# Layer 2 of a four-layer graph kernel: a ring of four quads of weight parts, and the group's inverses, scalings and finish one quad later

## The chip, the cores and the metric

One Trainium2 core runs the whole kernel. The metric is the device time of one execution in microseconds, the median of several runs. The engines are named PE (TensorE), DVE (VectorE), ACT (ScalarE), POOL (GpSimd) and SP (SyncE); each has its own queue of instructions and runs it in order, and they wait for each other by semaphores.

## The reference

Four layers over 4096 nodes with 256 features and a 4096 x 4096 0/1 matrix `adj`. Each layer takes `h = relu(layernorm(x))` and adds a graph layer to `x`. The change is in layer 2, counted from 0, a graph attention:

```python
h = x @ W
e = (h @ a[:D, 0])[:, None] + (h @ a[D:, 0])[None, :]
e = jnp.where(e > 0, e, 0.01 * e)
attention = jax.nn.softmax(jnp.where(adj > 0, e, MASK_VAL), axis=1)
x = x + jax.nn.elu(attention @ h)
```

Layer 3, which follows, is an attention with queries, keys and values made of the new `h`. Its projections are made in the finish of layer 2.

## The kernel before

The 4096 rows are eight groups (`G`) of 512 rows (`GW`), the 4096 columns 32 tiles of 128, taken four at a time: `R = 4` tiles are a quad, and a group has `Q = 8` quads. `aggregate` (line 1879) runs once for layer 1 and once for layer 2 (`weighted`). For layer 2 a quad of a group goes over three engines:

- DVE makes the weights of each of the four tiles in fp32 (`p32`, line 2033: a maximum, times the mask), for which it has four buffers;
- ACT copies each to fp16, the high part (`ph`, line 1983), and DVE subtracts for the low part (`pl`, line 2042, "lo" in the semaphores);
- PE multiplies 128-column pieces of both with the values `V`, also in two parts: for each tile 4 x 3 matmuls of 257 columns (lines 2113, 2114, 2116) into banks 0 to 3, one bank for each 128 rows of the group. Column 257 is the sum of the weights.

`ph` and `pl` have room for two quads: ACT's copy of a tile waits until PE has ended the same tile two quads before (line 1982). PE takes the last quad of a group by rows (`quad_by_rows`), so that bank 0 is complete first and bank 3 last.

When a group's sums are complete, DVE inverts the weights' sum of each bank (`inverse`, `rden`, line 2060) and ACT scales the bank into `ag` (line 2004). PE's first quad of the next group uses the same banks, and waits for `ag` of each bank (`act_s.before(g, "ag", i)` in `quad`). What follows is the finish, `finish_layer2`: `below` and `e` on ACT (the exponential of the negative part, lines 2413 and 2416), `pos` and `x` on DVE (2439, 2444) into `xo`, the moments for the layernorm (1853, 1857, 1859), `rstd` on POOL, `nb` (1871) on DVE, `h` on ACT (2184), its transposes on PE (211), their high part on ACT and low part on DVE (`hT`, 2178 and 2174), the projections on PE (`qT` and `v`, line 193), and their high and low parts again (`qT`, `v`, 2178 and 2174).

The finish of group g - 1 runs inside the loop over group g. The order is written out: in `groups` each engine does `quad(g, q)` and then `part(eng, g - 1, q)`, for q from 0 to 7, and the functions `act_part`, `dve_part`, `dve_middle` (between a quad's `p32` and its `lo`), `pe_part` and `sync` say with `if q == ...` which step belongs behind which quad. Before the change `inverse` and `ag` are behind quad 0 (the last bank's inverse inside quad 1, between its second and third `p32`); `below` at 0; `e`, `pos`, `x` and moments at 1; `nb`, `h` and the transposes at 2; `hT` at 4; the projections at 5; `qT` and `v` at 7. The last group's finish comes after the loop, with no quads between its steps. Group 0 comes before the loop, and in it ACT and DVE also make the two parts of `V` (lines 1996, 2047).

Of the kernel before, what the change touches and what calls it, by code (L numbers as in the profile page):

```python
# [21 lines left out]
F32 = mybir.dt.float32  # L22
F16 = mybir.dt.float16
# [8 lines left out]
P = 128  # L32
# [82 lines left out]
def build(nc, a, out):  # L115
# [20 lines left out]
    with top:  # L136
# [1746 lines left out]
        def aggregate(V, side, slope=None, wh=None):  # L1883
# [8 lines left out]
            v_at = v_row if weighted else v_own  # L1892
            with ExitStack() as mem, nc.Block() as block:
                mask = sb(mem, "mask", [P, MS, R * GW], U8)
                ph = sb(mem, "ph", [P, 2 * R, GW], F16)
                ag = sb(mem, "ag", [P, R * D], F32)
                rden = sb(mem, "rden", [P, R], F32)
                if weighted:
                    p32 = sb(mem, "p32", [P, R, GW], F32)
                    pl = sb(mem, "pl", [P, 2 * R, GW], F16)  # L1900
                    gam = sb(mem, "gam2", [P, T], F32)
                    dtil = sb(mem, "dtil", [P, T], F32)
                    red = sb(mem, "red", [P, 1], F32)
                    reded, d_spread, dmaxed, dtiled, lifted = (Count(sem(f"l2_{n}")) for n in (
                        "d_reduced", "d_spread", "d_max", "d_shifted", "s_lifted"))
                    omega_x, gam_x, v_x, omega_s, gam_s, v_col = (Count(sem(f"l2_{n}")) for n in (
                        "omega_exp", "gam_exp", "v_exp", "omega_scaled", "gam_scaled", "v_column"))
                    gam_spread, gam_rowed, v_hi, v_lo = (Count(sem(f"l2_{n}")) for n in (
                        "gam_spread", "gam_rowed", "v_hi", "v_lo"))
# [8 lines left out]
                masks = 16 * loaded[0]  # L1918

                def slot(q, r):  # L1920
                    return (q % 2) * R + r

                def mask_here(g, q):
                    return s_mask[q % MS], g * (16 * Q // MS) + (masks + 16 * (q // MS + 1))
# [48 lines left out]
                @block.scalar  # L1973
                def _(act):
                    def quad(g, q):
                        if not weighted:
                            act.wait_ge(*mask_here(g, q))
                        for r in range(R):
                            if weighted:
                                act.wait_ge(dve_q.sem, dve_q.at(g * Q + q, "p32", r))  # L1980

                            act.wait_ge(pe_q.sem, pe_q.before(g * Q + q, "pv", r, 2))
                            nc.scalar.copy(ph[:, slot(q, r), :], p32[:, r, :] if weighted else  # L1983
                                           mask[:, q % MS, r * GW:(r + 1) * GW]
                                           ).then_inc(act_q.sem, act_q.one("hi", r))

                    def gam_row(q):
                        act.wait_ge(gam_spread.sem, gam_spread.upto(q))
                        nc.scalar.copy(s_row[:, q * GW:(q + 1) * GW], bank[4 + q % R][:, :]).then_inc(gam_rowed.sem, 1)  # L1989

                    def make(q):

                        if q + 1 < Q:
                            gam_row(q + 1)
                        for t in range(q * R, q * R + R):
                            nc.scalar.mul(v_row(V, 0, t, D), wh[:, t * D:(t + 1) * D], vprime[:, t:t + 1]
                                          ).then_inc(v_hi.sem, 1)

                    def part(act, g, q):
                        if q == 0:  # L2000
                            work["sums_free"](act, g)
                            for r in range(R):
                                act.wait_ge(dve_s.sem, dve_s.at(g, "rden", r))
                                nc.scalar.mul(row(ag, r), bank[r][:, 0:D], rden[:, r:r + 1]
                                              ).then_inc(act_s.sem, act_s.one("ag", r))
                        work["act"](act, g, q)

                    if weighted:
                        act.wait_ge(dtiled.sem, dtiled.upto(0))
                        nc.scalar.activation(omega[:, :], dtil[:, :], ACT.Exp, scale=1.0 - slope  # L2010
                                             ).then_inc(omega_x.sem, 1)
                        act.wait_ge(lifted.sem, lifted.upto(0))
                        nc.scalar.activation(gam[:, :], gam[:, :], ACT.Exp, scale=slope - 1.0).then_inc(gam_x.sem, 1)
                        nc.scalar.activation(vprime[:, :], dtil[:, :], ACT.Exp, scale=slope).then_inc(v_x.sem, 1)
                        act.wait_ge(v_x.sem, v_x.upto(0))
                        nc.scalar.copy(v_column(V, 0), vprime[:, :]).then_inc(v_col.sem, 1)
                        gam_row(0)
                    groups(act, quad, part, make if weighted else None, work.get("act_between"), work.get("act_beside"))

                @block.vector  # L2020
                def _(dve):
                    def quad(g, q):
                        if not weighted:
                            return
                        n = g * Q + q
                        dve.wait_ge(*mask_here(g, q))
                        if isinstance(g, int):
                            dve.wait_ge(gam_rowed.sem, gam_rowed.upto(q))
                        for r in range(R):
                            dve.wait_ge(dve_q.sem, dve_q.before(n, "lo", r))  # L2030
                            if r == 2 and q == 1 and not isinstance(g, int):
                                inverse(g - 1, R - 1, R)
                            nc.vector.scalar_tensor_tensor(  # L2033
                                out=p32[:, r, :], in0=s_row[:, ds(g * GW, GW)],
                                scalar=omega[:, q * R + r:q * R + r + 1],
                                in1=mask[:, q % MS, r * GW:(r + 1) * GW], op0=ALU.max, op1=ALU.mult
                                ).then_inc(dve_q.sem, dve_q.one("p32", r))
                        if not isinstance(g, int):
                            middle(g - 1, q)
                        for r in range(R):  # L2040
                            dve.wait_ge(act_q.sem, act_q.at(n, "hi", r))
                            nc.vector.tensor_tensor(pl[:, slot(q, r), :], p32[:, r, :], ph[:, slot(q, r), :],  # L2042
                                                    ALU.subtract).then_inc(dve_q.sem, dve_q.one("lo", r))
                        if isinstance(g, int):
                            for t in range(q * R, q * R + R):
                                dve.wait_ge(v_hi.sem, v_hi.upto(t))
                                nc.vector.scalar_tensor_tensor(
                                    out=v_row(V, 1, t, D), in0=wh[:, t * D:(t + 1) * D], scalar=vprime[:, t:t + 1],
                                    in1=v_row(V, 0, t, D), op0=ALU.mult, op1=ALU.subtract).then_inc(v_lo.sem, 1)
# [17 lines left out]
                    def part(dve, g, q):  # L2067
                        if isinstance(g, int) or not weighted:
                            middle(g, q)
                        if q == 0:  # L2070
                            inverse(g, 0, R if isinstance(g, int) or not weighted else R - 1)
                        work["dve"](dve, g, q)

# [285 lines left out]


        def finish_layer2(mem, ag):
            xg = sb(mem, "xg4", [P, R * D], F32)
            xo = sb(mem, "xo2", [P, R * D], F32)
            e = w_gate[0][:, 0:2 * R * D].bitcast(F32)
            h = w_gate[1][:, 0:2 * R * D].bitcast(F32)
            qT = sb(mem, "qTg", [P, 2, K, GW], F16)
            stx, mvx, vex, rsx = stats_tiles(mem, "x2")
            nb = sb(mem, "nb4", [P, R], F32)
            pe_s.plan(("hT", K), ("qT", K), ("v", R))
# [38 lines left out]
                                    ).then_inc(s_xout, 16)  # L2408

            def act_part(act, g, q):  # L2410
                if q == 0:
                    act.wait_ge(act_s.sem, act_s.at(g, "ag", R - 1))
                    nc.scalar.activation(e[:, :], ag[:, :], ACT.Relu, scale=-1.0).then_inc(act_s.sem, act_s.one("below"))
                if q == 1:
                    act.wait_ge(act_s.sem, act_s.at(g, "below"))
                    nc.scalar.activation(e[:, :], e[:, :], ACT.Exp, scale=-1.0).then_inc(act_s.sem, act_s.one("e"))
                if q == 2:
                    normal(act, g, h, xo, nb, rsx)
                if q == 4:
                    act.wait_ge(pe_s.sem, pe_s.at(g, "hT", K - 1))  # L2420
                    hi(columns(kT[0], g), psum[:, 4:6, :], "hT", 0)
                if q == 7:
# [4 lines left out]
                    hi(own_values(0, g), made_values(), "v", 0)  # L2427

            def dve_middle(dve, g, q):
                if q == 2:  # L2430
                    shift(dve, g, nb, mvx, rsx, "nb", "rx")

            def dve_part(dve, g, q):
                if q == 1:

                    dve.wait_ge(act_s.sem, act_s.at(g, "ag", R - 1))
                    dve.wait_ge(s_xin, g * 16 + (first_in + 16))
# [7 lines left out]
                                                   op0=ALU.add, op1=ALU.add).then_inc(dve_s.sem, dve_s.one("x"))  # L2445
                    moments(dve, g, [(row(xo, r), None) for r in range(R)], stx, mvx, vex, ("xs", "xm", "xv"),
                            (dve_s.sem, dve_s.at(g, "x")))
                if q == 4:
                    dve.wait_ge(act_s.sem, act_s.at(g, "hT"))
                    lo(columns(kT[1], g), psum[:, 4:6, :], columns(kT[0], g), "hT", 0)  # L2450
                if q == 7:
# [3 lines left out]
                    lo(own_values(1, g), made_values(), own_values(0, g), "v", 0)  # L2455

            def pe_part(pe, g, q):
                if q == 2:

                    pe.wait_ge(dve_s.sem, dve_s.before(g, "v"))  # L2460
                    for k in range(K):
# [381 lines left out]
```

## Time and profile before

| | us |
|---|---|
| median of 3 runs | 2376.57 (2375.01 to 2377.3) |
| the profiled execution | 2376.45 |
| its span | 2374.8 |
| PE busy | 2227.9 (94%) |
| DVE busy | 1801.5 (76%) |
| ACT busy | 1373.3 (58%) |
| layer 2, first `p32` to last matmul into the sums | 1225.7 to 1645.8 |

The span is from the first to the last instruction. Busy time counts an engine's instructions; matmuls are pipelined, so that one matmul of 257 columns is listed with 0.27 us where the next starts 0.11 us later. A line of the timeline gives start, length, engine, line, operation, output and inputs with shapes, and in brackets the idle time before it and who ended it. Several like instructions in a row are merged (`x4`). The granted clock is 1.00 at 2.4 GHz and 0.50 at 1.2 GHz.

### The profile page before, as it was taken

The page shows a single profiled execution, that of the slowest core. Times are in us where ns is not written, and L with a number is a line of the kernel's source. Part 1 is how long each engine was busy: PE and PEld are TensorE (multiplying, and loading weights), DVE is VectorE, ACT ScalarE, POOL GpSimd, SP SyncE. Part 2 cuts the span into 40 slices and gives each one's busy share as a digit, 9 for nine tenths or more (in the row PEclk, how much of TensorE's full clock was granted, in tenths as well). Part 3 has the DMA queues.
Part 4 walks back from the last instruction along what each step waited for, and adds up shares of the span by engine and source line. Part 5 has one row for each costly group of instructions (what it writes and reads, how often), then busy time and mean ns, then how long its engine had stood idle before and what let it go on. Part 6 is the DMA issues. An engine that isn't in the chain of part 4 may idle for free. (4 is left out here: it accounts for less than half of the span.)

```text
span 2374.8 us, 45610 instructions
## 1 busy us (share of the span) xinstructions
PE 2227.9 (94%) x17180; PEld 1703.0 (72%) x17180; DVE 1801.5 (76%) x2845; ACT 1373.3 (58%) x2100; POOL 114.6 (5%) x124
## 2 busy tenths in 40 slices
PE   5899999999999998999978999997899999999998
PEld 4677767777677776888867888886356666666667
DVE  6967778696877855211259999997698898898896
ACT  6655564655646565666655555554365565565556
POOL 2000010010100001000000000000000000000000
PEclk9899999999999999999989999998999999999999
DMA  7542240414321112222211222221211111111000
GB/s 176 112 63 46 54 85 28 81 45 81 56 61 46 38 57 81 84 91 87 88 41 56 69 66 77 77 66 45 84 36 32 45 54 50 33 48 50 23 32 27
DMA packets 62934, 146.72 MB, mean 62 GB/s; under 512 B 10023, under 2 KB 14778, under 8 KB 61757
## 3 DMA queue, kind: packets, MB, share of 16 engines
q1 hardware_dynamic: 56461, 110.57, 14.8%
q0 software_dynamic: 5760, 33.56, 8.6%
q8 instruction: 100, 1.64, 0.3%
q10 hardware_dynamic: 560, 0.52, 0.1%
q14 instruction: 53, 0.43, 0.1%
HBM read 170.30 MB, written 41.43 MB: 89 GB/s over the span
## 5 line engine op out<-in xcount | busy, mean ns | idle before, releaser
L2113 PE MATMUL bank<-VB,ph 128*128 128x257 f16 x1936 | 487.6, 275 | 37.6 <-DVE pl L2042 19.9
L2114 PE MATMUL bank<-VB,ph 128*128 128x257 f16 x1936 | 486.6, 275 | 0.0
L193 PE MATMUL bank<-s_row,kT_hi 128*128 128x512 f16 x1024 | 305.5, 380 | 10.5 <-DMA s_row<-qT_d 8.6
L1559 PE MATMUL bank<-VA,ph 128*128 128x257 f16 x1024 | 280.8, 274 | 6.8 <-DVE VA L1168 6.8
L2770 PE MATMUL bank<-VA,w_dense 128*128 128x257 f16 x1024 | 280.7, 274 | 3.0 <-ACT w_dense L2631 2.4
L2116 PE MATMUL bank<-VB,pl 128*128 128x257 f16 x1024 | 281.4, 275 | 0.0
L1561 PE MATMUL bank<-VA,pl 128*128 128x257 f16 x1024 | 280.5, 274 | 0.0
L1560 PE MATMUL bank<-VA,ph 128*128 128x257 f16 x1024 | 280.5, 274 | 0.0
L2772 PE MATMUL bank<-VA,pl 128*128 128x257 f16 x1024 | 280.2, 274 | 0.0
L2771 PE MATMUL bank<-VA,w_dense 128*128 128x257 f16 x1024 | 280.1, 274 | 0.0
L1983 ACT CAST ph<-p 128x512 f16<-128x512 f32 x256 | 155.8, 617 | 153.5 <-DVE p L2033 144.1
L2113 PEld LDWEIGHTS bank<-VB,ph 128*128 128x128 f16 x1936 | 189.9, 98 | 69.2 <-DVE pl L2042 25.4
L811 ACT CAST ph<-p 128x512 f16<-128x512 f32 x256 | 153.2, 618 | 147.1 <-DVE p L1154 144.1
L2114 PEld LDWEIGHTS bank<-VB,ph 128*128 128x128 f16 x1936 | 190.7, 98 | 25.0
L193 PE MATMUL bank<-s_row,kT_lo 128*128 128x512 f16 x512 | 194.6, 380 | 0.0
L1154 DVE SCALAR_TENSOR_TENSOR p<-gamr,omega,mask 128x512 f32<-128x512 f32 x256 | 180.3, 747 | 2.5 <-ACT gamr L820 2.4
L193 PEld LDWEIGHTS bank<-s_row,kT_hi 128*128 128x128 f16 x1024 | 100.2, 98 | 110.9 <-DMA s_row<-qT_d 8.8
L2033 DVE SCALAR_TENSOR_TENSOR p<-s_row,omega,mask 128x512 f32<-128x512 uint8 (+1 forms) x256 | 175.8, 751 | 2.5 <-ACT s_row L1989 2.4
L1163 DVE TENSOR_TENSOR pl<-p,ph 128x512 f16<-128x512 f32 x256 | 165.0, 686 | 1.4 <-ACT ph L811 1.4
L2042 DVE TENSOR_TENSOR pl<-p,ph 128x512 f16<-128x512 f32 x256 | 159.9, 692 | 6.7 <-ACT ph L1983 6.7
L2607 ACT ACTIVATE s_row<-mask 128x1024 bf16<-128x1024 uint8 x128 | 134.1, 1053 | 34.3 <-DVE scores L2659 12.7
L1983 ACT CAST ph<-mask 128x512 f16<-128x512 uint8 x228 | 123.9, 622 | 8.8 <-DMA mask<-mask_d 5.1
(338 smaller groups left out, 4543.2 us busy)
## 6 DMA issues: line engine op xcount, KB each, us to landing
mask<-mask_d SPq DMA_DIRECT2D x256, 256.0 KB, 2.7
mask_d<-in_adj POOLq DMA_DIRECT2D x8, 2048.0 KB, 23.2
xg<-x SPq DMA_DIRECT2D x16, 512.0 KB, 4.3
x<-xo POOLq DMA_DIRECT2D x16, 512.0 KB, 3.0
xg<-in_x SPq DMA_DIRECT2D x8, 512.0 KB, 12.7
x<-xg SPq DMA_DIRECT2D x8, 512.0 KB, 3.9
qT_d<-qTg POOLq DMA_DIRECT2D x8, 512.0 KB, 2.9
s_row<-qT_d SPq DMA_DIRECT2D x8, 512.0 KB, 4.2
```

Source lines behind the costliest of these rows:

```text
L193: last = nc.tensor.matmul(out_ap, st, mv, start=(i == 0), stop=(i == len(todo) - 1))
L1154: nc.vector.scalar_tensor_tensor(out=p32[:, u % PR, :], in0=gamr[:, g % 2, :], scalar=omega[:, t:t + 1], in1=mask[:, n % MS, (u % R) * GW: ...
L1559: nc.tensor.matmul(acc, ph[:, u % HR, c], v_row(V, 0, t), start=(t == 0), stop=False)
L1560: nc.tensor.matmul(acc, ph[:, u % HR, c], v_row(V, 1, t), start=False, stop=False)
L1561: last = nc.tensor.matmul(acc, pl[:, u % HR, c], v_row(V, 0, t), start=False, stop=(t == T - 1))
L1983: nc.scalar.copy(ph[:, slot(q, r), :], p32[:, r, :] if weighted else mask[:, q % MS, r * GW:(r + 1) * GW]).then_inc(act_q.sem, act_q.one(" ...
L2113: nc.tensor.matmul(acc, p_hi, v_at(V, 0, t), start=first, stop=False)
L2114: last = nc.tensor.matmul(acc, p_hi, v_at(V, 1, t), start=False, stop=final and not weighted)
L2116: last = nc.tensor.matmul(acc, pl[:, slot(q, r), c], v_at(V, 0, t), start=False, stop=final)
L2770: nc.tensor.matmul(acc, ph[:, u % ring, j, c], v_row(V, 0, t), start=(t == 0), stop=False)
L2771: nc.tensor.matmul(acc, ph[:, u % ring, j, c], v_row(V, 1, t), start=False, stop=False)
L2772: last = nc.tensor.matmul(acc, pl[:, u % ring, j, c], v_row(V, 0, t), start=False, stop=(t == T - 1))
```

## The change

`ph` and `pl` of layer 2 get room for four quads, and ACT's copy waits for PE's tile of four quads before. `late = 1` moves `inverse` and `ag` behind quad 1, and the last bank's inverse into quad 2. In the finish, `below` goes to 1, where `e` already is; `pos`, `x` and moments to 2; `nb`, `h` and the transposes to 3; `hT` to 5. The projections (5) and `qT`, `v` (7) stay. `xg`, `xo` and `qT` have no tiles of their own any more and lie in a part of `w_dense` that is not used at that time. Layer 1 keeps its ring of two and its order.

```diff
+                ring = 4 if weighted else 2
+                late = 1 if weighted else 0
+                ph = sb(mem, "ph", [P, ring * R, GW], F16)
-                    pl = sb(mem, "pl", [P, 2 * R, GW], F16)
+                    pl = sb(mem, "pl", [P, ring * R, GW], F16)
                 def slot(q, r):
-                    return (q % 2) * R + r
+                    return (q % ring) * R + r
-                            act.wait_ge(pe_q.sem, pe_q.before(g * Q + q, "pv", r, 2))
+                            act.wait_ge(pe_q.sem, pe_q.before(g * Q + q, "pv", r, ring))
                     def part(act, g, q):
-                        if q == 0:
+                        if q == late:
                             work["sums_free"](act, g)
-                            if r == 2 and q == 1 and not isinstance(g, int):
+                            if r == 2 and q == 1 + late and not isinstance(g, int):
                                 inverse(g - 1, R - 1, R)
                     def part(dve, g, q):
-                        if q == 0:
+                        if q == late:
                             inverse(g, 0, R if isinstance(g, int) or not weighted else R - 1)
         def finish_layer2(mem, ag):
-            xg = sb(mem, "xg4", [P, R * D], F32)
-            xo = sb(mem, "xo2", [P, R * D], F32)
+            spare = dense_all[:, 2 * sizes[2]:2 * sizes[2] + 6 * R * D]
+            xg = spare[:, 0:2 * R * D].bitcast(F32)
+            xo = spare[:, 2 * R * D:4 * R * D].bitcast(F32)
-            qT = sb(mem, "qTg", [P, 2, K, GW], F16)
+            qT = spare[:, 4 * R * D:6 * R * D].rearrange("p (a k n) -> p a k n", a=2, k=K)
             def act_part(act, g, q):
-                if q == 0:
+                if q == 1:
                     act.wait_ge(act_s.sem, act_s.at(g, "ag", R - 1))
...
-                if q == 2:
+                if q == 3:
                     normal(act, g, h, xo, nb, rsx)
-                if q == 4:
+                if q == 5:
                     act.wait_ge(pe_s.sem, pe_s.at(g, "hT", K - 1))
             def dve_middle(dve, g, q):
-                if q == 2:
+                if q == 3:
                     shift(dve, g, nb, mvx, rsx, "nb", "rx")
             def dve_part(dve, g, q):
-                if q == 1:
+                if q == 2:
...
-                if q == 4:
+                if q == 5:
                     dve.wait_ge(act_s.sem, act_s.at(g, "hT"))
             def pe_part(pe, g, q):
-                if q == 2:
+                if q == 3:
...
```

## Rows read from the trace of the kernel before

**Rows 1.** Busy time by stretch: us, engines' busy (x instructions), clock, DMA
```profile
1388.10:1439.20 51.10, 48.67 (x430) 41.74 (x429) 48.83 (x84) 27.99 (x45) 2.60 (x3) 1.00 0.22 72
```
**Rows 2.** Waits, layer 2: who waited for whom, us, times, longest
```profile
PE bank L2113 <- DVE pl L2042: 19.9, 8, 3.0
DVE rden L2060 <- PE bank L2116: 13.9, 11, 3.6
...
ACT ph L1983 <- PE bank L2116: 2.5, 1, 2.5
```
**Rows 3.** Timeline of PE, round that begins at 1391.63 (group 3)
```profile
1391.63 0.28 PE L2113 MATMUL bank<-VB,ph 128*128 128x257 f16 x1
...
1401.11 0.27 PE L2116 MATMUL bank<-VB,pl 128*128 128x257 f16 x1
1403.81 0.28 PE L2113 MATMUL bank<-VB,ph 128*128 128x257 f16 x1 [2.43 <-DVE pl L2042]
...
1431.06 0.27 PE L2113 MATMUL bank<-VB,ph 128*128 128x257 f16 x1
```
**Rows 4.** Timeline of DVE, the same round
```profile
1389.46 0.17 DVE L2060 RECIPROCAL rden<-bank 128x1 f32<-128x1 f32 x1 [1.07 <-PE bank L2116]
...
1393.20 2.50 DVE L2042 TENSOR_TENSOR pl<-p,ph 128x512 f16<-128x512 f32 x4 [0.82 <-ACT ph L1983]
1395.62 1.22 DVE L2439 SCALAR_TENSOR_TENSOR xo<-ag,xg 128x1024 f32<-128x1024 f32 x1
...
1400.34 2.74 DVE L2033 SCALAR_TENSOR_TENSOR p<-s_row,omega,mask 128x512 f32<-128x512 uint8 x4
```
**Rows 5.** Timeline of ACT, the tail after the last group
```profile
1646.80 1.06 ACT L2413 ACTIVATE w_gate<-ag 128x1024 f32<-128x1024 f32 x1
1647.88 1.06 ACT L2416 ACTIVATE w_gate<-w_gate 128x1024 f32<-128x1024 f32 x1
```
**Rows 6.** Timelines of DVE, ACT and PE, border of groups 0 and 1
```profile
1280.38 2.74 DVE L2033 SCALAR_TENSOR_TENSOR p<-s_row,omega,mask 128x512 f32<-128x512 uint8 x4
...
1285.44 0.43 DVE L2060 RECIPROCAL rden<-bank 128x1 f32<-128x1 f32 x3
...
1285.63 1.20 ACT L2004 ACTIVATE ag<-bank,rden 128x256 f32<-128x256 f32 x3 [1.80 <-DVE rden L2060]
1287.34 0.47 ACT L2004 ACTIVATE ag<-bank,rden 128x256 f32<-128x256 f32 x1 [0.50 <-DVE rden L2060]
...
1286.71 0.27 PE L2116 MATMUL bank<-VB,pl 128*128 128x257 f16 x1
...
1287.86 0.28 PE L2113 MATMUL bank<-VB,ph 128*128 128x257 f16 x1
```
**Rows 7.** Timelines of PE, ACT and DVE at `v`, round of group 1
```profile
1328.94 0.27 PE L2113 MATMUL bank<-VB,ph 128*128 128x257 f16 x1
...
1329.23 1.01 ACT L2178 CAST VA<-bank 128x1024 f32 x1 [1.71 <-PE bank L193]
...
1330.45 1.23 DVE L2174 TENSOR_TENSOR VA<-bank,VA 128x1024 f32 x1 [1.11 <-ACT VA L2178]
1331.59 2.73 DVE L2033 SCALAR_TENSOR_TENSOR p<-s_row,omega,mask 128x512 f32<-128x512 uint8 x4
```
**Rows 8.** Timeline of PE, group 7: the gated matmul and the last
```profile
1595.87 0.28 PE L2113 MATMUL bank<-VB,ph 128*128 128x257 f16 x1
...
1645.78 0.27 PE L2116 MATMUL bank<-VB,pl 128*128 128x257 f16 x1
```
**Rows 9.** Busy time by stretch after holes of PE (clock after POOL), and PE's timeline
```profile
1300.10:1303.50 3.40, 3.40 (x17) 2.41 (x18) 3.40 (x6) 2.81 (x6) 0.00 (x0) 0.51 0.44 137
1352.75:1356.15 3.40, 3.40 (x31) 3.03 (x32) 3.40 (x6) 2.81 (x6) 0.00 (x0) 1.00 0.46 145
...
1300.54 0.42 PE L2113 MATMUL bank<-VB,ph 128*128 128x257 f16 x1
1300.75 0.42 PE L2114 MATMUL bank<-VB,ph 128*128 128x257 f16 x1
```

More of the change, by code:

```diff
@@ L1894, in aggregate @@
                 mask = sb(mem, "mask", [P, MS, R * GW], U8)
-                ph = sb(mem, "ph", [P, 2 * R, GW], F16)
+                ring = 4 if weighted else 2
+                late = 1 if weighted else 0
+                ph = sb(mem, "ph", [P, ring * R, GW], F16)
                 ag = sb(mem, "ag", [P, R * D], F32)
```

## The prediction

> **What bounds it now.** I read three kinds of view, in this order. The page and the busy times by stretch come first: in one round of layer 2 (51.1 us: eight quads of one group, with the finish of the group before between them) PE is busy 48.67 us and DVE 48.83 us, ACT only 27.99 us [rows 1]. Two engines are both nearly full, so which of them waits, and where, decides. Next, the waits: of the whole stretch of layer 2 the largest one of PE's matmuls is for the low parts, 19.9 us in 8 waits, and DVE's largest is `rden` for PE, 13.9 us [rows 2]. Last the timelines of one round, engine by engine. PE stops once a round, from 1401.22 (one matmul pitch of 0.11 after the last) to 1403.81, 2.59 us, before the low parts of quad 2 [rows 3]. DVE is late there because in that quad it has computed `pos`, `x` and the moments (1395.62 to 1400.34, 4.72 us) [rows 4]. And DVE itself stood idle 1.07 us at the third `rden` (PE had not ended that row) and 0.82 us before the low parts of quad 1, where ACT's copies were behind `ag` and `below` [rows 4]. So the round is one closed chain of both engines: PE from quad 2 to the end of quad 7, DVE from the inverses to the low parts of quad 2. The matmul let go by the fourth `ag` starts at 1391.63 in group 3 and at 1595.87 in group 7 [rows 3, 8]: 204.24 us for four rounds, 51.06 each. PE alone would need 51.06 - 2.59 = 48.47.
>
> **The change, part by part.**
>
> (1) Ring of four quads. It adds no instruction. What it lifts is ACT's wait for PE before a high part: 2.5 us, one time, in the whole layer [rows 2], on an engine with 23 us of idle time a round. Worth nothing by itself; what it makes possible is that DVE and ACT run further ahead of PE.
>
> (2) `inverse` and `ag` one quad later. The same four reciprocals and four scalings, but now queued on DVE behind the four `p32` and four `lo` of quad 1 (5.06 us, 1280.38 to 1285.44 [rows 6]), and on ACT behind the high parts of quad 1. Who waits: PE's quad 0 of the next group accumulates into the same banks 0 to 3 and waits for `ag` bank by bank; only `dve` and `act` are moved, not the sums' place. So PE can't begin quad 0 before DVE has ended quad 1. Before, its wait there was too short for the list of waits. This is an added wait of PE, and all of quads 0 to 7 is queued behind it.
>
> (3) The finish one quad later. `pos`, `x`, moments go from quad 1 to 2 on DVE, the transposes from 2 to 3, `hT` from 4 to 5; the projections stay in quad 5, `qT` and `v` in quad 7. Same instructions, so no work is added. `below` moves into quad 1 beside `e`, and both now stand ahead of the high parts of quad 2. Before, `below` alone did. `e` waits for `below`, and starts 1.08 us after it in the tail, where nothing is between them (1646.80 and 1647.88) [rows 5]; that much later the high parts start. DVE's 0.82 us idle becomes 1.90.
>
> (4) `xg`, `xo`, `qT` in the spare part of `w_dense`: same shapes, same instructions, 0. SP's load of `xg` and POOL's stores keep their place; SP runs four quads ahead of DVE, so that load is still issued before it is wanted.
>
> **The new round, step by step.** D is the start of the first reciprocal. In group 1, where nothing held DVE up, the first reciprocal (1285.44) to PE's matmul that waits for the fourth `ag` (1287.86) took 2.42 us [rows 6]; call that matmul the gate.
> - Gate to the first matmul of quad 6, after the projections: 1391.63 to 1431.06, less the stall of 2.59: 36.84 us [rows 3]. The stall is gone: DVE has done quad 2 long before.
> - ACT takes `v` 0.29 us after that matmul (1328.94 to 1329.23), DVE's `lo` of `v` 1.22 later (1330.45): the one round in which DVE waited for them [rows 7].
> - DVE then goes on 1.14 us later (1331.59) with the `p32` of quad 0 [rows 7], and two quads of `p32` and `lo` take twice 5.06, 10.12 us [rows 6]. Here is the next D.
>
> Sum: 2.42 + 36.84 + 0.29 + 1.22 + 1.14 + 10.12 = **52.03 us a round**, against 51.06. Is another chain longer? DVE by itself: 51.06, less the 1.07 us for which it waited in the inverses [rows 4], and 1.08 more for ACT: 51.07. So DVE comes to `v` 0.96 us too early and waits. PE by itself: 48.47. The chain over both is the longest. A check of PE against DVE within the round, counted from D: PE's quads are 48 matmuls of 0.11, 5.3 us, and nine of the first stand before the gate, so quad 3 starts at 2.4 - 1.0 + 3 x 5.3 = 17.3. DVE needs 2.8 + 0.3 us for `p32` and inverses and 1.9 idle to the low parts of quad 2, 2.4 for these, 4.7 for the finish (both [rows 4]) and 2.7 for the next `p32`: low parts of quad 3 from 14.8. They are 2 us ahead of PE, and in quads 4 and 5 DVE gains 0.2 more each. So PE has no stall inside the group.
>
> **From rounds to the end of the layer.** D of group 1: `p32` of quad 0 starts at 1280.38 [rows 6] and two quads take 10.12: 1290.50, gate at 1292.92. Before, it was 1287.86. Six rounds: 1292.92 + 312.18 = 1605.10 is the gate of group 7, then PE needs 1645.78 - 1595.87 - 2.59 = 47.32 us to its last matmul [rows 8]: 1652.42, before 1645.78. **+6.6 us.** The tail (last inverse, finish of group 7) is in the same order as before, 0, with some 1.7 us either way for the clock, below.
>
> **PE's clock.** The change turns a hole of 2.4 us into one of 52.03 - 2.42 + 0.71 - 47.32 - 0.27 = 2.73 us (0.71 from D to the first matmul: 0.19 to `ag`, 0.52 to PE [rows 6]), with 0.6 us more before the gate. After ten holes of 2.4 to 3.0 us the granted clock of the next 3 to 4 us was 0.50 to 0.58 (1.2 GHz all or most of the time) four times, from 1232, 1280, 1300 and 2323 us, and 1.00 (2.4 GHz) six times, in the six steady rounds [rows 9] (one of the four and one of the six stand there). In the low stretch 17 matmuls stand 0.21 apart instead of 0.11 [rows 9]: 1.7 us. No row says why some holes are followed by a fall, and the new ones are no shorter. I take the ratio, four in ten, of six holes: 2.4 x 1.7 = 4.1 us, bounds 0 and 10.2. The first hole is longer: PE ends quad 7 of group 0 at 1286.98 [rows 6] and would start at 1291.21, 4.2 us. I expect a low stretch, partly hidden by the waits for `ag`: 1.0, bounds 0 and 1.9.
>
> **Sum:** 6.6 + 4.1 + 1.0 = +11.7 us. The profiled execution took 2376.45 (span 2374.8 and 1.65 around it), 0.12 under the median 2376.57, so its like after the change is 2388.15, a span of 2386.5, and the median 2388.3 us.
>
> **Rivals.**
> - A, the forecast: 2388.3, own range 2384 to 2393. 56%.
> - B, the chain as above, but the clock stays: +6.6 to +7.3, 2383.5. For it: six steady holes in a row without a fall. Against: the two just before them fell. 16%.
> - C, a fall after every hole: 6.6 + 10.2 + 1.9 = +18.7, 2395.3. 10%.
> - D, the way over `v` is shorter than I make it (PE goes through its matmuls a microsecond faster, or DVE's lead is larger) and only DVE's own chain is left: 6 x 51.07 gives the gate of group 7 at 1599.34, +3.5, less the 2.59 of the last round: +0.9, 2377.5. 11%.
> - E, the other side: the hole of PE goes and none comes in its place, 7 x 2.59 = 18 us, 2358.5. The mechanism would be that DVE has a lead of more than two quads at the group's border, so that `ag` is ready when PE ends quad 7. The point from which this decides: DVE's work with its waits in a round must be under PE's 48.47 us. It is 51.07, of which 48.83 is bare work [rows 1], and any lead is lost each round. 7%, for what I can't see, half gains included.
>
> For E speaks a rule of the Trainium skill, Perfetto Trace Analysis, section Optimization Strategy: the same bubble repeating on an engine that should be saturated can mean that there are too few buffers for the next tile. The bubble here does repeat in all seven rounds [rows 2, 3], and by the rule a deeper ring would take it away and give 2358.5. But the rows name DVE's work, not a buffer, as what ends it.
>
> **Numbers.** A run of this kernel can tell about 0.2% (4.75 us) from no change, so slower is above 2381.3. A, B and C are slower but for a part of B's lower edge: 0.80. D is the same, with some of B: 0.13. Faster is E: 0.07. The range 2379.5 to 2395.5 holds A, B, C nearly whole and leaves out D and E.
>
> **What would show it.** After the change: no PE idle before quad 2; in its place PE idle of about 2.7 us before quad 0 of every group, ended by ACT `ag`; `rden` no longer waiting for PE inside the loop; DVE idle of about 1.9 us before the low parts of quad 2, ended by ACT `ph`; DVE `lo` of `v` waiting about 1 us for ACT (more after a low clock); rounds of 52.0 us at a clock of 1.00, and some of 53.7 with a stretch at half of it. Step 2 is wrong if PE's idle before quad 0 is absent; the sum is wrong if the `v` wait is absent (then D); and if rounds are below 49 us, E holds.

## The result, and the profile after

The changed kernel takes 2389.3 us (median of 5 runs, 2387.71 to 2390.97), the kernel before 2376.57 (median of 5, 2375.01 to 2378.76). The ratio is 1.0054, with a 95% interval of 1.0043 to 1.0066: slower by 12.7 us. The profiled execution took 2389.3 with a span of 2387.6 us, 12.8 more than before's 2374.8. The forecast was 2388.3 us, with a span of 2386.5.

The first view is the page of the changed kernel; its lines answer to the table ahead of the prediction.

```profile
span 2387.6 us, 45610 instructions
PE 2233.9 (94%) x17180; PEld 1704.2 (71%) x17180; DVE 1800.5 (75%) x2845; ACT 1373.7 (58%) x2100; POOL 114.6 (5%) x124
L2115 PE MATMUL bank<-VB,ph 128*128 128x257 f16 x1936 | 489.4, 276 | 44.1 <-ACT ag L2006 26.1
```

The count of instructions is the same and the busy times are nearly so: no work was added. What changed is who ends PE's idle time before the matmuls of the sums. Before, it was DVE's low parts [rows 2]; now it is ACT's `ag`. (Lines were added to the kernel, so L2113 of before is L2115, L2116 is L2118, L2042 is L2044, L2060 is L2062, L2004 is L2006, and the high and low parts of `qT` and `v`, L2178 and L2174, are L2180 and L2176. A tile that is now listed as `w_dense` is one of the three that moved there: `xg`, `xo` or `qT`.)

Next, one round of the changed kernel that has no low clock in it, from the first reciprocal of group 4 to that of group 5 (1449.43 to 1501.26 us, 51.83). The waits in it that matter here, with us in total, times, longest:

```profile
PE bank L2115 <- ACT ag L2006: 3.0, 2, 2.7
ACT ag L2006 <- DVE rden L2062: 2.1, 2, 1.8
DVE pl L2044 <- ACT ph L1985: 1.9, 1, 1.9
ACT VA L2180 <- PE bank L193: 1.5, 1, 1.5
DVE VA L2176 <- ACT VA L2180: 0.8, 1, 0.8
```

Against [rows 2], `rden` does not wait for PE any more and PE does not wait for `pl`. The new waits are the four that were said: PE for `ag`, DVE for `ph`, and DVE for `v` with ACT's wait for PE ahead of it. Their places are seen in the timelines of PE, ACT and DVE, in this order:

```profile
1450.15 0.28 PE L2115 MATMUL bank<-VB,ph 128*128 128x257 f16 x1 [2.73 <-ACT ag L2006]
...
1451.67 0.28 PE L2115 MATMUL bank<-VB,ph 128*128 128x257 f16 x1 [0.29 <-ACT ag L2006]
...
1488.50 0.27 PE L2115 MATMUL bank<-VB,ph 128*128 128x257 f16 x1
...
1488.79 1.01 ACT L2180 CAST VA<-bank 128x1024 f32 x1 [1.51 <-PE bank L193]
...
1449.43 0.29 DVE L2062 RECIPROCAL rden<-bank 128x1 f32<-128x1 f32 x3
...
1490.00 1.22 DVE L2176 TENSOR_TENSOR VA<-bank,VA 128x1024 f32 x1 [0.82 <-ACT VA L2180]
1491.14 2.73 DVE L2035 SCALAR_TENSOR_TENSOR p<-s_row,omega,mask 128x512 f32<-128x512 uint8 x4
...
1501.26 0.29 DVE L2062 RECIPROCAL rden<-bank 128x1 f32<-128x1 f32 x3
```

Read it as the chain of the prediction, where D is the first reciprocal and the gate is PE's matmul that waits for the fourth `ag`: D at 1449.43, the gate at 1451.67 (2.24 us), the first matmul of quad 6 at 1488.50 (36.83), ACT at `v` at 1488.79 (0.29), DVE at 1490.00 (1.21), the `p32` of quad 0 at 1491.14 (1.14), the next D at 1501.26 (10.12). The sum is 51.83.

The seven rounds do not all look like this. The first reciprocals of the eight groups start at 1289.51, 1343.45, 1396.06, 1449.43, 1501.26, 1553.08, 1606.45 and, after the loop, 1652.33 us: rounds of 53.94, 52.61, 53.37, 51.83, 51.82 and 53.37, then 45.88 with nothing of a next group behind it. The long ones begin with a stretch of low clock (the column after POOL's), at 0.50 or 0.52:

```profile
1290.20:1295.70 5.50, 5.48 (x26) 3.87 (x27) 3.59 (x8) 5.12 (x9) 0.00 (x0) 0.50 0.17 48
1344.20:1347.00 2.80, 2.80 (x14) 1.98 (x15) 2.25 (x5) 2.42 (x5) 0.00 (x0) 0.52 0.00 0
1398.10:1401.50 3.40, 3.20 (x16) 2.25 (x17) 1.49 (x3) 3.34 (x6) 0.00 (x0) 0.50 0.26 77
1450.15:1453.50 3.35, 3.06 (x26) 2.26 (x27) 2.27 (x5) 2.97 (x5) 0.00 (x0) 1.00 0.00 0
1502.00:1505.40 3.40, 3.11 (x27) 2.30 (x28) 2.25 (x5) 3.02 (x5) 0.00 (x0) 1.00 0.00 0
1555.10:1558.50 3.40, 3.18 (x15) 2.24 (x16) 1.49 (x3) 3.34 (x6) 0.00 (x0) 0.50 0.26 76
1607.20:1610.60 3.40, 3.11 (x27) 2.30 (x28) 2.24 (x5) 3.02 (x5) 0.00 (x0) 1.00 0.00 0
```

From the first `p32` to the end of the last matmul into the sums, layer 2 took 420.36 us before (1225.69 to 1646.05) and 431.57 now (1224.70 to 1656.27): +11.2. It began 1.0 us earlier, and what lies behind it took 731.4 instead of 728.7, +2.7. These two make up the rest of the 12.8.

### The profile page after: what moved, and what is told of

The parts are those of the page before. It is cut to its first block and busy times, and to the rows that moved or that the text cites. A ratio compares the mean times of both kernels' runs of the same rounds, so it can differ in the third digit from the quotient of the medians.

```text
span 2387.6 us, 45610 instructions
## 1 busy us (share of the span) xinstructions
PE 2233.9 (94%) x17180; PEld 1704.2 (71%) x17180; DVE 1800.5 (75%) x2845; ACT 1373.7 (58%) x2100; POOL 114.6 (5%) x124
## 5 line engine op out<-in xcount | busy, mean ns | idle before, releaser
L2115 PE MATMUL bank<-VB,ph 128*128 128x257 f16 x1936 | 489.4, 276 | 44.1 <-ACT ag L2006 26.1
L2116 PE MATMUL bank<-VB,ph 128*128 128x257 f16 x1936 | 488.1, 276 | 0.0
L2118 PE MATMUL bank<-VB,pl 128*128 128x257 f16 x1024 | 283.2, 277 | 0.0
L2115 PEld LDWEIGHTS bank<-VB,ph 128*128 128x128 f16 x1936 | 190.4, 98 | 77.8 <-ACT ag L2006 31.2
L2116 PEld LDWEIGHTS bank<-VB,ph 128*128 128x128 f16 x1936 | 191.3, 99 | 25.6
L2044 DVE TENSOR_TENSOR pl<-p,ph 128x512 f16<-128x512 f32 x256 | 159.3, 682 | 14.3 <-ACT ph L1985 14.3
## 6 DMA issues: line engine op xcount, KB each, us to landing
xg<-in_x SPq DMA_DIRECT2D x8, 512.0 KB, 12.6
```

The lines of the kernel that those rows point to most:

```text
L2115: nc.tensor.matmul(acc, p_hi, v_at(V, 0, t), start=first, stop=False)
L2116: last = nc.tensor.matmul(acc, p_hi, v_at(V, 1, t), start=False, stop=final and not weighted)
L2118: last = nc.tensor.matmul(acc, pl[:, slot(q, r), c], v_at(V, 0, t), start=False, stop=final)
```

## The experiments

The theory is that a round is the chain D, gate, PE to the projections, `v` on ACT and DVE, two quads on DVE, and that PE's low clock lengthens it. The rivals: the ring's depth matters by itself; the high parts that ACT makes late, behind `below` and `e`, set the round; the later steps of the finish cost, not the later inverses.

**The ring alone** (`ring_only`). Against the changed kernel the late inverses are undone, and in the finish every step that was moved goes back by one (`below`, `h` and `hT` on ACT; `nb`, the step with `x`, and `hT` on DVE; the transposes on PE). Each is an edit like the second pair of lines:

```diff
-                late = 1 if weighted else 0
+                late = 0
...
-                if q == 1:
+                if q == 0:
                     act.wait_ge(act_s.sem, act_s.at(g, "ag", R - 1))
```

> The ring of four quads and the moved tiles alone, with inverse, ag and every step of the finish where they were before. My theory: the ring hides nothing, since PE's hole before quad 2 is ended by DVE's work. The hole of 2.4 us stays in every round, rounds of 51.06, and the time is that of before, 2376.6 (within 2 us). Rival (too few buffers make the hole): the hole goes, rounds near 48.5, 2358.5.

Measured: 2376.34 us, ratio 1.0002 (0.9993 to 1.0011). Rounds of 51.06, as before, and the hole is in its place. PE's waits in the layer:

```profile
PE bank L2115 <- DVE pl L2044: 20.1, 8, 3.1
```

Against 19.9 us in 8 waits [rows 2]. Two more quads of buffers and the three moved tiles are worth nothing alone. With this falls the reading that the repeated bubble comes of too few buffers, which the Trainium skill, Perfetto Trace Analysis, section Optimization Strategy, names as a possible cause. Here the bubble stayed, and `late_undone` below makes it shorter by another order.

**`below` and `e` out of the way** (`exp_later`):

```diff
             def act_part(act, g, q):
-                if q == 1:
+                if q == 2:
                     act.wait_ge(act_s.sem, act_s.at(g, "ag", R - 1))
...
-                if q == 1:
+                if q == 2:
                     act.wait_ge(act_s.sem, act_s.at(g, "below"))
```

> The changed kernel with below and e behind the high parts of quad 2 instead of ahead of them. My theory (the round is the chain gate, PE to the projections, v on ACT and DVE, two quads on DVE): DVE's 1.91 us idle before the low parts of quad 2 goes, DVE's wait for v grows by the same, the clean round stays 51.8 and the time stays 2389 (within 2.5). Rival (ACT's wait is what lengthens the round): rounds of 49.9, 6 x 1.9 = 11 us less, 2378.

Measured: 2388.45 us, ratio 1.0055 (1.0041 to 1.0068); clean rounds of 51.83. The waits of the one from 1394.03 to 1445.86:

```profile
PE bank L2115 <- ACT ag L2006: 3.0, 2, 2.7
...
DVE VA L2176 <- ACT VA L2180: 1.7, 1, 1.7
DVE w_dense L2176 <- ACT w_dense L2180: 1.1, 1, 1.1
```

DVE's 1.9 us before the low parts of quad 2 is gone, and as much has come at `v` (0.8 to 1.7) and at `qT` (0 to 1.1; the line with `w_dense`). So that visible wait could go without shortening the round: the chain over PE set it. In this run's profile two of the six steady holes were followed by a low clock, not three, and not the same ones: its long rounds are the first (53.87), the fourth (53.40) and the last (47.44 instead of 45.88).

**The projections one quad earlier** (`project_earlier`):

```diff
             def pe_part(pe, g, q):
...
-                if q == 5:
+                if q == 4:
                     pe.wait_ge(dve_s.sem, dve_s.at(g, "hT"))
```

> The changed kernel with PE's projections behind quad 4 instead of quad 5, so that v is ready 5.3 us earlier. My theory: DVE no longer waits for v (0.8 to 1.7 us a round before), DVE's own chain is left, clean rounds of 51.0, and a low clock of PE costs nothing inside the loop, since DVE no longer waits for PE: 6 x 0.8 + about 4 = 9 us less than the changed kernel, 2380.5 (2378 to 2385). Rival (ACT's wait alone sets the round): no change, 2389.

Measured: 2376.66 us, ratio 1.0001 (0.9992 to 1.0010), which is no difference from the kernel before and 12.6 us less than the changed one. Rounds: 50.90, then five of 50.93. The direction and the round were right (51.0), but the time is below my range of 2378 to 2385. The changed rounds add up to 316.94 us and these to 305.55, 11.4 less, where I had put 9: the low clock in the changed rounds cost 6.0 and not 4. The stretch behind the layer, 728.7 instead of 731.4, does the rest. The waits of the round from 1442.94:

```profile
PE bank L2115 <- ACT ag L2006: 2.0, 2, 1.7
DVE pl L2044 <- ACT ph L1985: 1.9, 1, 1.9
```

PE still waits for `ag`, and that wait costs nothing now, since nothing waits for PE in turn. Even the hole of 5.7 us before group 1, with a low clock behind it, left a round of 50.90:

```profile
1291.00:1296.00 5.00, 5.00 (x24) 3.49 (x25) 3.09 (x7) 4.62 (x9) 0.00 (x0) 0.50 0.17 52
```

What is left on the chain is DVE with its 1.9 us of waiting for ACT, as the next run shows.

**Both edits** (`both_moved`), the two diffs above together.

> Both edits together on the changed kernel: below and e behind the high parts of quad 2, projections behind quad 4. My theory: neither the way over v nor ACT's wait is left, DVE's bare work is, clean rounds of 49.1 to 49.2; against the changed kernel 6 x 2.7 = 16 us and the clock's 4, so 2369 (2366 to 2373), under the kernel before. Rival (one of the two alone sets the round): the time of the better single edit.

Measured: 2365.26 us, ratio 0.9953 (0.9940 to 0.9967): 11 us under the kernel before, and 0.7 under my range of 2366 to 2373, with rounds of 48.92 where I had put 49.1. DVE's waits between 1290 and 1632 us:

```profile
DVE rden L2062 <- PE bank L2118: 7.0, 1, 7.0
DVE kT_lo L2176 <- ACT kT_hi L2180: 1.6, 1, 1.6
DVE st_x L1853 <- DVE w_dense L2447: 0.9, 6, 0.2
DVE mv_x L1857 <- DVE st_x L1853: 0.8, 5, 0.2
```

The first is after the loop. The second is in the first round (50.57), behind the first hole and its low clock. In the other rounds DVE waits for no other engine: they hold its bare work and 0.3 us between its own instructions. This is the floor under this order of steps, 0.45 above PE's own 48.47. Of the edits alone, `exp_later` was worth 0 us a round and `project_earlier` 0.9, both together 2.9. There are two chains of nearly the same length, and the one that isn't edited keeps what is taken from the other from showing.

**The hole filled** (`hole_filled`). PE gets 24 matmuls whose result is not used, ahead of quad 0:

```diff
+                        if weighted and q == 0 and not isinstance(g, int):
+                            pe.wait_ge(dve_s.sem, dve_s.before(g, "v", 0, 2))
+                            for _ in range(24):
+                                nc.tensor.matmul(bank[7][:, 0:D + 1], ones16[:, :], v_at(V, 0, 0), start=True, stop=True)
```

> The changed kernel with 24 more matmuls of 257 columns on PE ahead of quad 0 of each group after the first, into a bank that is free then; their result is not used. They are 24 x 0.11 = 2.6 us, about the hole of 2.7, so PE stays busy up to the first ag and the quad starts no later. My theory: the rounds above 51.83 (53.95, 52.61, 53.37 and 53.37 in the changed kernel's profile, 5.9 us in all) are low clock after the hole; with it filled all rounds but the first are 51.8 and the kernel takes 4 to 6 us less, 2384. Rival (the hole has nothing to do with the falls, or something else lengthens those rounds): rounds of 52.6 to 54 remain and the time is 2389.

Measured: 2383.78 us, ratio 1.0022 (1.0013 to 1.0031). Rounds: 53.49, then 51.82, 51.83, 51.82, 51.83, 51.83. PE's waits for `ag` after 1300 us, and the clock at two of the borders:

```profile
PE bank L2115 <- ACT ag L2006: 1.7, 6, 0.3
...
1342.00:1346.00 4.00, 3.62 (x32) 2.51 (x30) 2.81 (x7) 3.61 (x6) 0.00 (x0) 1.00 0.01 2
1394.00:1398.00 4.00, 3.63 (x32) 2.51 (x30) 2.63 (x5) 3.62 (x7) 0.00 (x0) 1.00 0.05 7
```

All the long rounds but the first are gone, and layer 2 takes 427.26 us instead of 431.57, 4.3 less. More work on PE made the kernel faster: the slowest of its 11 runs (2384.35) is below the fastest of the changed kernel's five (2387.71). So the low clock makes the rounds long, and the holes bring it on. The first hole was 5.7 us and is still 3.1 with the filling, and its round is still long.

**The later inverses undone** (`late_undone`). Only this of the change goes back; ring and finish stay:

```diff
-                late = 1 if weighted else 0
+                late = 0
```

> The changed kernel with inverse and ag back behind quad 0; the ring of four and the finish's steps one quad later stay. My theory: PE no longer waits at the group's border, so the chain over v falls away; DVE's work for pos, x and moments now stops PE before quad 3 instead of quad 2, one quad (5.28 of PE, 5.06 of DVE) later, and below and e no longer hold up ACT's copies, which takes 0.8 us of DVE's idle time off. Rounds of about 50.2, 6 us less than before the change, 2370 (2368 to 2373). So the added wait before quad 0 costs some 19 us against this. Rival (the finish's steps one quad later are what costs): 2389 or at least above 2380.

Measured: 2369.84 us, ratio 0.9965 (0.9951 to 0.9978), faster than before by 8 us and than the changed kernel by some 20. Rounds of 49.91, where I had put 50.2. PE's stall is before quad 3 and is 1.28 instead of 2.43 us, and DVE's wait for the third row is 0.84 instead of 1.07 [rows 4]:

```profile
1453.93 0.28 PE L2115 MATMUL bank<-VB,ph 128*128 128x257 f16 x1 [1.28 <-DVE pl L2044]
...
1434.38 0.22 DVE L2062 RECIPROCAL rden<-bank 128x1 f32<-128x1 f32 x2
1435.44 0.17 DVE L2062 RECIPROCAL rden<-bank 128x1 f32<-128x1 f32 x1 [0.84 <-PE bank L2118]
```

So of the change's parts the inverses one quad later are the whole loss and more, and the finish one quad later is a gain. That gain is measured with the ring of four in place; no run has it with a ring of two.

**The third inverse beside the fourth** (`inverse_split`), on top of the last one:

```diff
-                                inverse(g - 1, R - 1, R)
+                                inverse(g - 1, R - 2, R)
...
-                            inverse(g, 0, R if isinstance(g, int) or not weighted else R - 1)
+                            inverse(g, 0, R if isinstance(g, int) or not weighted else R - 2)
```

> The kernel with inverse and ag back behind quad 0, and besides the third bank's inverse moved beside the fourth's, between the second and third p32 of quad 1, so that DVE does not stand before the third row (0.85 us a round there). My theory: that idle goes, about 0.2 us of waiting for the high parts comes, DVE's bare work of 48.9 sets the round: 49.2 instead of 49.9, 7 x 0.7 = 5 us less, 12 to 13 us under the kernel before, a ratio of 0.9945 to 0.995. Rival (DVE's idle there is slack and PE sets the round): 49.9 and a ratio of 0.9965.

Measured: 2365.76 us, ratio 0.9949 (0.9935 to 0.9962). The time is the one that I gave, but not for my reason. The rounds are 49.80, not 49.2. DVE's wait has only moved from the third row to the fourth:

```profile
1434.58 0.16 DVE L2062 RECIPROCAL rden<-bank 128x1 f32<-128x1 f32 x1
1435.52 0.17 DVE L2062 RECIPROCAL rden<-bank 128x1 f32<-128x1 f32 x1 [0.78 <-PE bank L2118]
```

DVE still waits for PE to end a row of quad 7, now the last one. In the profiled executions layer 2 took 409.96 us against 410.69 of `late_undone`, 0.7 less; the layer began 1.0 us earlier, and the rest took 728.7 instead of 731.7 us, with one low stretch of the clock less in it, at 1716 us. By these two executions, about 3 of the 4 us between the two medians lie outside layer 2, where the two kernels are the same: a right number by luck.

## Why the prediction was right

The sign, the mechanism and the place came out as written: PE waits for `ag` at the group's border and no longer inside the group, and DVE waits for `v`. `late_undone` shows that the later inverses are the loss. The median came out within 1 us, which is closer than the terms are. The sum, term by term:

- **The clean round.** Forecast 52.03, measured 51.83. The term that was off is the first, D to gate: 2.42 forecast, 2.24 measured. I had taken it from group 1 of before [rows 6], and there the three reciprocals took 0.43 us and the fourth began 1.70 after the first; here it is 0.29 and 1.52. The prediction says that nothing held DVE up there, and this reading was probably wrong: PE's rows were ending at that time (the last at 1286.98, one row is 12 matmuls of 0.11), so the third reciprocal, due at about 1285.6, would have waited for its row. All the others are within 0.01. That is 1.2 us less over six rounds, and 0.2 at the first gate: of +6.6 some 5.2 are left. `hole_filled` shows this round by itself, five times.
- **The low clock after the holes.** Forecast 2.4 falls of 1.7, 4.1 us. There were three after six holes of 2.73 us, and they cost 0.78, 1.54 and 1.54 (the rounds less 51.83), 3.9 us. The first is cheaper since part of it lay under the waits for `ag`: it began with the first matmul at 1344.2 and ended at 1347.0, and only what lies behind the gate at 1345.7 counts.
- **The first hole.** Forecast 4.2 us of idle and a cost of 1.0, at most 1.9. It was 5.72 us and cost 2.1 (53.94 less 51.83). My error: PE ran quad 7 of group 0 at full clock this time (it ended at 1284.51, before at 1286.98), since the low stretch after the hole at 1279 did not come; so the hole began earlier. The bound was too small.
- **Layer 2 in all.** 5.2 + 3.9 + 2.1 = 11.2, measured 11.2, forecast 11.7.
- **Outside the layer** I put 0 with 1.7 either way. It was +2.7 behind it and -1.0 ahead of it, 1.7 together. The sum came within 1 us by luck in part: the clean round's -1.4 offsets half of the first hole's +1.1 and of these 1.7.
- **DVE's own chain**, 51.07 forecast for the case that the way over `v` is out: `project_earlier` has 50.93, and the 1.90 us of ACT in it is 1.91. That chain, taken as rival D with 11%, is a real floor, and it was 0.9 us under the round, as worked out (0.96).
- **Rival E** fell. `ring_only` has the deeper ring and keeps the hole. But its condition, a round of DVE not longer than PE's 48.47, can nearly be had: `both_moved` has 48.92, and then the late inverses cost PE only 0.3 us at the border. The prediction's statement that DVE's 51.07 forbids it was true of the change as it stands, and no more.

The +2.7 behind the layer, which I had as noise, goes with the clock too. PE at the same place of both kernels, first changed, then before:

```profile
1734.31 0.66 PE L211 MATMUL bank<-ident,w_dense 128*128 128x128 f32 x4 [1.12 <-DVE w_dense L2680]
1736.12 1.01 PE L193 MATMUL bank<-s_row,kT_hi 128*128 128x512 f16 x2 [1.16 <-DVE m_col L2685]
...
1723.04 0.66 PE L211 MATMUL bank<-ident,w_dense 128*128 128x128 f32 x4 [1.12 <-DVE w_dense L2677]
1724.86 0.59 PE L193 MATMUL bank<-s_row,kT_hi 128*128 128x512 f16 x2 [1.16 <-DVE m_col L2682]
```

In the changed kernel the clock is 0.50 from 1736.0 to 1739.4 us, in the one before it stays at 1.00. Of the nine profiled executions five have such a low stretch between 1716 and 1740 us (`after`, `ring_only`, `exp_later`, `hole_filled`, `late_undone`), and what lies behind layer 2 takes 731.3 to 732.2 us in them; the four without it take 726.5 to 728.7. That goes together in all nine, but no run changes it on purpose.

What stays open is why the same hole is followed by a low clock one time and not the next: three of six holes of 2.73 us in the changed kernel, two of six in `exp_later`, none of the six of 2.4 us in the steady rounds of before. These counts are of one profiled execution each. The 21 runs of the kernel before that stand beside `ring_only` go from 2374.57 to 2380.53 us, and their mean granted clock from 0.983 down to 0.979, so the number of falls differs from execution to execution, and the forecast's 2.4 falls were a rate and no mechanism.

## What to carry to other kernels

When two engines hand work to each other in a loop, write the round as closed chains, one for each way round, and compare the change with the second longest too: here it was 0.9 us away, so either edit alone gave at most that, and both gave 2.9. Moving a step later in one engine's order moves everyone who waits for its result. A deeper ring lets a producer run ahead, but the accumulators' banks were not doubled, so here the consumer had to wait until the producer was two quads ahead. Where a step is moved to give slack, ask what it frees: the finish's steps were worth moving (49.91 us a round instead of 51.06), the inverses, which free the banks, were not.

## What the runs showed of the hardware

In layer 2 the granted clock fell after holes of PE of 2.4 to 2.7 us, but not after each: three times of six in the changed kernel, two times of six in `exp_later`, never in the six steady rounds of before, and not once at the borders of `hole_filled` after the first. Behind the layer it fell after two holes of 1.12 and 1.16 us in the changed kernel, and not after the same two in the kernel before. A fall in a steady round cost 0.8 to 1.5 us where others waited for PE; the one in `project_earlier`, where nobody did, cost nothing.

The Trainium skill's page TensorE: Matmul & The Clock Gate, section HAM oscillation, describes a kernel whose PE waits some 3 to 5 us for a DMA in each tile and starts every next tile cold. The trace agrees in kind, but here shorter waits, and waits for other engines, were enough, and in some rounds only.

Filling the hole with 24 idle matmuls a round (2.6 us of PE) won 4.3 us in layer 2. An order that leaves almost no hole is better still, by 16 us as the ratios 1.0022 and 0.9953 stand; most of that is the shorter round, 48.92 instead of 51.83, and not the clock.
